# One clear per run of adjacent semaphore numbers in a two-stage kernel's `clear`

## The reference

```python
x = L0_attn_x                                   # (32, 256, 128), float32
x = x + LN(attention(LN(x)))                    # 16 heads, q and k of width 4, normalised, values of width 64,
                                                # a learnt bonus per key, causal softmax
x = x + LN(ternary_ffn(LN(x)))                  # silu(x w1) * (x w2), two 512x512 gelu layers, back to 128
x = x + LN(rnn(LN(x)))                          # h = tanh(x_t Wi + h Wh + b), 256 steps for a batch of 32
x = x + LN(shared_swiglu(LN(x)) + routed(LN(x)))  # top-1 of 32 experts, scaled by sigmoid of the winning logit
```

## Time and profile before

| what | us |
|---|---|
| median of three runs | 1968.08 |
| lowest and highest | 1967.4 and 1968.75 |
| the profiled execution | 1965.75 |
| its span, from the first to the last instruction | 1964.0 |

### The profile page before, as it was taken

The page is one execution under the profiler, slowest core; times in us unless marked ns, Lnnn a source line. Parts: engine busy times, 40 slices in busy tenths (PEclk is TensorE's granted clock), DMA queues, the critical chain, the costliest instruction groups (busy, mean ns, idle before and its releaser), DMA issues. The chain is left out here.

```text
span 1964.0 us, 43536 instructions
## 1 busy us (share of the span) xinstructions
PE 1709.4 (87%) x12768; PEld 1243.7 (63%) x12768; DVE 1328.3 (68%) x4113; ACT 887.3 (45%) x1955; POOL 999.6 (51%) x1825
## 2 busy tenths in 40 slices
PE   4999999999999999848899999999999998568884
PEld 3566666666666666536777777777777775335552
DVE  6777777777777777634556666666666656457774
ACT  2655555555555555414444444444444443123331
POOL 5777777777777777722223333333333332237775
PEclk8999999999999999969999999999999998679997
DMA  1011111111111112010110000000001005034431
GB/s 38 10 50 49 48 48 45 41 37 46 48 48 48 48 48 94 12 33 17 54 54 28 28 28 28 28 27 27 27 27 32 22 22 188 33 105 124 121 114 26
DMA packets 78237, 95.73 MB, mean 49 GB/s; under 512 B 7046, under 2 KB 62995, under 8 KB 78160
## 3 DMA queue, kind: packets, MB, share of 16 engines
q1 hardware_dynamic: 70992, 77.91, 12.9%
q0 software_dynamic: 7168, 16.87, 2.4%
HBM read 53.14 MB, written 43.69 MB: 49 GB/s over the span
## 5 line engine op out<-in xcount | busy, mean ns | idle before, releaser
L644 ACT ACTIVATE wgu<-score 128x384 f32<-128x384 f32 x512 | 223.1, 489 | 100.1 <-PE score L468 94.9
L313 POOL TENSOR_SCALAR_AFFINE_SELECT wgu<-wgu 128x512 f32<-128x512 f32 x256 | 164.3, 642 | 152.9 <-ACT wgu L644 144.3
L1228 PE MATMUL main<-hT_high,h_high 128*128 128x512 f32 x512 | 231.9, 453 | 0.9 <-ACT hT_high L1437 0.9
L1230 PE MATMUL main<-hT_high,h_low 128*128 128x512 f32 x512 | 204.6, 400 | 0.0
L491 PE MATMUL outp<-wgu 128*64 128x256 f32 (+1 forms) x2048 | 196.0, 334 | 0.9 <-POOL wgu L313 0.8
L491 PEld LDWEIGHTS outp<-wgu 128*64 128x64 f32 x2048 | 127.8, 137 | 58.1 <-issue 17.1
L1139 POOL TENSOR_TENSOR hT_low<-wgu,hT_high 128x512 fp32r<-128x512 f32 x64 | 82.2, 1285 | 151.5 <-ACT wgu L1424 151.4
L1679 DVE SCALAR_TENSOR_TENSOR th<-th,main 128x512 f32<-128x512 f32 x64 | 43.9, 685 | 156.3 <-ACT th L1468 156.3
L1237 PE MATMUL main<-hT_low,h_high 128*128 128x512 f32 x512 | 139.1, 393 | 0.1
L525 PE MATMUL back<-wout,wgu 128*128 128x128 f32 x1024 | 131.7, 283 | 0.0
L786 DVE TENSOR_TENSOR wgu<-spread,wgu 128x512 f32<-128x512 f32 x128 | 87.0, 680 | 61.1 <-PE spread L511 56.0
(11 more groups left out here) (270 smaller groups left out, 4244.3 us busy)
## 6 DMA issues: line engine op xcount, KB each, us to landing
sorted_d<-row_buf SPq DMA_DIRECT2D x26, 772.0 KB, 3.7
xg<-sorted_d SPq DMA_DIRECT2D x48, 386.0 KB
wgu<-in_gate_up SPq DMA_DIRECT2D x4, 2048.0 KB, 10.8
xa<-in_x SPq DMA_DIRECT2D x32, 128.0 KB, 3.5
xr<-in_x SPq DMA_DIRECT2D x32, 128.0 KB, 3.2
x_d<-x SPq DMA_DIRECT2D x32, 128.0 KB, 1.9
x1c<-x_d SPq DMA_DIRECT2D x16, 256.0 KB
x1v<-x_d SPq DMA_DIRECT2D x16, 256.0 KB
```

The costliest lines, as they stand in the source:

```text
L313: pool.affine_select(out=blocks, in_=blocks, compare_op=ALU.is_ge, fill=0.0, base=0, pattern=[[0, 4], [1, P]], channel_multiplier=-1).then ...
L644: act.activation(prob[:, h // 2 % (RING // 2), :, h % 2, :], score[h % BANKS][:, 0:SC].rearrange("p (c q) -> p c q", q=P), ACT.Exp).then_i ...
L1228: pe.matmul(main[m % 2][:, :], w[0][:, k, m * P:(m + 1) * P], src[0][:, k, :], start=(k == 0), stop=False)
L1230: pe.matmul(main[m % 2][:, :], w[1][:, k, m * P:(m + 1) * P], src[0][:, k, :], start=False, stop=False)
```

## The change

`clear` first sorts the numbers of the semaphores. It then goes through them with their successors and, wherever the successor is not the next number, issues one `sem_clear` with the `range` of numbers from the run's first to its last. Before, it issued a `sem_clear` for each semaphore. Both calls of `clear` are affected; nothing else in the program is edited.

```diff
 def clear(nc, sems):
 
+    numbers = sorted(sem.num for sem in sems)
     with nc.Block() as block:
         @block.gpsimd
         def _(pool):
-            for sem in sems:
-                pool.sem_clear(sem)
+            first = numbers[0]
+            for here, following in zip(numbers, numbers[1:] + [None]):
+                if following != here + 1:
+                    pool.sem_clear(range(first, here + 1))
+                    first = following
```

## The result

Before 1968.08 us (median of 5 executions, 1964.99 to 1972.1), after 1951.73 us (5, 1949.04 to 1955.75). The medians are 16.35 us apart; the ratio, taken over the executions and not from the medians, is 0.9922 with a 95% interval of 0.9905 to 0.9939, that is 15.4 us faster, between 12.0 and 18.7. (Beside the experiments further down, one execution of before took 4059.52 us; it is left out of every figure.)

What follows compares the result with a forecast made beforehand. Not the busiest engine but two groups of clears, 12.58 us with nothing else running, were taken to hold all up. Gains of 5.14 and 7.32 us, called 12.4, off 1968.08 gave 1955.7, range 1954.3 to 1962.8.

Steps and rivals of the forecast that it cites:

- bare, and on the path: Clears at attention's end and program's end: nothing else runs for 5.20 + 7.38 = 12.58 us, and everything that follows waits.
- what is issued: In `clear`: one instruction in place of 76 at attention's end, one in place of 110 at the program's end.
- the cover: Two instruction fetches under attention's clears, the only work there; up to 1.8 us could be uncovered, nothing taken.
- the prediction's own sign: From L63's release to PE's first matmul stays 6.9 us if the clears covered nothing; longer means they covered the fetches.
- Rival D: POOL's later loops refetch code after its code shortens, 1.8 us a miss; slower, up to 1992; chance 0.02.
- the length of the range would cost nothing: Price of each new range clear, lower end: 38 ns in its record, 64 ns to the next, whatever the count.
- rival B: Sequencer walks the range in both clears, 21 to 38 ns a number; 1959.6 to 1962.8 us; chance 0.34.
- A: The forecast: clears at both places cost per instruction; 1955.7 us, own range 1954.5 to 1957; chance 0.60.
- The estimate of 29 ns a number: Skill page's reset of 51 semaphores in about 1.5 us, read as one walk; would put the result near 1961.
- for the spread of the runs: 0.7 us in the forecast's own range, for three runs of before between 1967.4 and 1968.75 us.
- PE's clock ... at most 0.5 us either way: Clock rise after PE's first matmul behind attention's end may shift against PE's work; 0.5 us, in the range only.
- C: No gain: each number costs most of 64 ns, or the runs of numbers are broken; 1964.2 to 1968.1; chance 0.04.

Runs made afterwards that it cites:

- attention's half: Kernel before, with one range clear at attention's end only and 110 single clears kept at the program's end; ratios 0.9976, 0.9968, 0.9978 against before.
- the end's half: Kernel before, with one range clear at the program's end only and 76 single clears kept at attention's end; ratios 0.9968 and 0.9965 against before.
- the doubled pause: Kernel before, with each of attention's semaphores cleared twice, 152 single clears, program's end as before; ratio 1.0024, 4.8 us slower than before.

## Why the prediction was wrong

**Right: bare, and on the path.** Both groups of clears were taken as time in which nothing else runs and for which all wait. 4.72 and 6.72 us went, and attention's half and the end's half each moved the time by that.

**Right: what is issued, and the cover.** One instruction for each run of numbers. The stretch from the load to PE's first matmul was to stay 6.9 us; it was 6.8 to 6.9 in the five traces with single clears at attention's end and 7.0 to 7.2 in the nine of the changed kernel and attention's half. By the prediction's own sign something was covered, but 0.2 us and not 1.8. L914's long drain stayed (11.22 us). Rival D, loops that refetch, did not come up. The page of the changed kernel counts no more packets of instruction fetches than before's, which has 40 and 37:

```profile
q8 instruction: 40, 0.66, 0.1%
q14 instruction: 36, 0.29, 0.0%
```

**Wrong: "the length of the range would cost nothing".** The records are 38 ns for 1 number, 67 for 6, 306 for 51, 445 for 76, 632 for 110: (632 - 38) / 109 = 5.4 ns a number. The walk of rival B exists, at a quarter of the 21 ns that were its price. It takes 1.0 us of the 12.4, which is why A's sum was 12.46 and the stretches 11.4. The reason given for A, that the operation's name says range, was no evidence. The estimate of 29 ns a number, worked out from the Trainium skill, "Runtime: NRT & Kernel Launch", section "The ~15µs preamble/postamble breakdown", is five times the measured price. One range of 51 numbers took 306 ns here, where the section has about 1.5 us for its reset, so the two are not the same thing; no run here shows that reset.

**Wrong, and the step that put the time outside the range: the starting time 1968.08 with 0.7 us "for the spread of the runs", and "PE's clock ... at most 0.5 us either way".** The first took three runs of before that happened to lie within 1.4 us for the scatter, the second took the clock's effect from the one place at which the change touches it. The runs showed that executions of one kernel lie up to 14 us apart for before (1957.93 to 1971.52, 23 in one set) and 16 for the changed kernel (1944.76 to 1960.92), and that this follows the time PE spends at the low clock, 0.28 us a microsecond. The second stage alone took 1079.4 to 1086.1 us in nine traces with the same instructions.

The measured time is 4.0 us below 1955.7. Before's later 92 executions have a mean of 1965.3, so the starting time was 2.8 us too high. The walk costs 1.0 us the other way. The other 2.1 us are what this set of the changed kernel had beyond its stretches, which by the later sets goes with less time at the low clock. With a term of 2 us on each median the forecast's own range would have begun at 1954.5 - 2 = 1952.5, and the measured 1951.73 lies just below even that. Whether the change causes a part of the 2.1 stays open.

**The rivals.** B's mechanism is real at a lower price; C and D are out. None of them reached the measured side, as all rivals gave less than A. That the gain could exceed the stretches was considered nowhere. Three figures of it don't come out: 60 instructions more bring back 3.9 us and leave 8.5, which is B's time and not C's (C would need some 130), and A's terms add up to 1.8 us above 1955.7, which is 1957.5 and not 1957; A's low end is 1954.5 in one place and 1954.3 in the other.

## What to carry to other kernels

Work on a sequencer is in no busy share; look at barriers and ask what stands between them, for it is time of all engines. One clear for a range of semaphores costs about 32 ns and 5.4 ns a number, where single ones cost 64 ns each (71 in two kernels); 75 single ones in a pause in which POOL waited anyway cost nothing. Before a difference below 1% is read to the microsecond, repeat the kernel before against itself, and set each execution's time beside its granted clock: here five executions could not tell 11 us from 14, while the trace's stretches told 11.4 to the hundredth.

## What was unexpected of the hardware

With the same instructions a stage of 1085 us took 1079.4 to 1091.0 us in 20 traces; between the shortest and the longest the busy times of DVE, ACT and POOL differ by less than half a microsecond and PE's by 15, at a mean granted clock of 0.95 and 0.93. And a place in POOL's code costs 0.30 us when it is passed: it stood among the clears before, stood behind the release in the changed kernel, and came back into the stretch when eleven clears were issued. Among the 152 clears of the doubled pause it stood twice, 128 instructions apart.
